# A four-layer Macaron block on one Trainium2 core: the mixed layers' factor sums, bias additions and order of chunks

## The reference

```python
x = L0_attn_x
x = x + 0.5 * _L0_ffn_ref(_layernorm(x), W_r, b_r, W1, b1, W2, b2)      # routed: ffn_a
x = x + _L0_attn_ref(_layernorm(x), ...)                                # latent attention
x = x + 0.5 * _L0_ffn_ref(_layernorm(x), W_r, b_r, W1, b1, W2, b2)      # routed: ffn_b
x = x + 0.5 * _L1_ffn_ref(_layernorm(x), factors, bias)                 # mixed: mix_a
x = x + _L1_attn_ref(_layernorm(x), Wq, Wk, Wv, Wo)                     # attention
x = x + 0.5 * _L1_ffn_ref(_layernorm(x), factors, bias)                 # mixed: mix_b

def _layernorm(x, axis=-1, eps=1e-05):
    m = jnp.mean(x, axis=axis, keepdims=True)
    v = jnp.var(x, axis=axis, keepdims=True)
    return (x - m) / jnp.sqrt(v + eps)

def _L1_ffn_ref(x, factors, bias):           # factors: 8 x 256 x 256
    mixed = jnp.einsum('btd,rde->bte', x, factors)
    return mixed / math.sqrt(8) + bias
```

## Time and profile before

| | |
|---|---|
| median of 3 runs | 1937.31 us (1936.6 to 1941.16) |
| profiled execution, its own time | 1940.07 us |
| its span, first to last instruction | 1938.3 us |
| TensorE busy | 1717.4 us (89%) |
| VectorE busy | 1531.0 us (79%) |
| ScalarE busy | 1181.3 us (61%) |
| GpSimd busy | 983.2 us (51%) |
| mean granted clock of TensorE | 0.932 of full speed |

### The profile page before, as it was taken

The page is one execution under the profiler, slowest core; times in us unless marked ns, Lnnn a source line. Parts: engine busy times, 40 slices in busy tenths (PEclk is TensorE's granted clock), DMA queues, the critical chain, the costliest instruction groups (busy, mean ns, idle before and its releaser), DMA issues. The chain is left out here.

```text
span 1938.3 us, 27188 instructions
## 1 busy us (share of the span) xinstructions
PE 1717.4 (89%) x9368; PEld 1003.3 (52%) x9368; DVE 1531.0 (79%) x2236; ACT 1181.3 (61%) x2043; POOL 983.2 (51%) x820
## 2 busy tenths in 40 slices
PE   4667999999999999999999998565979899999986
PEld 3554555556565555565565654455644344444445
DVE  6772888998997988988889887677566988888816
ACT  1045787777776777778777776111325377778760
POOL 0004799897896997988979988002412000000110
PEclk8776999999999999999999999677987699999998
DMA  3100000000000000000000000111330200110001
GB/s 101 55 24 24 1 1 1 15 1 12 3 1 15 1 1 15 1 15 1 1 7 1 1 1 1 47 47 38 76 77 2 34 1 2 21 15 2 2 1 44
DMA packets 26697, 34.34 MB, mean 18 GB/s; under 512 B 5312, under 2 KB 19648, under 8 KB 26432
## 3 DMA queue, kind: packets, MB, share of 16 engines
q1 hardware_dynamic: 25360, 31.28, 6.8%
q10 hardware_dynamic: 1200, 1.31, 0.2%
HBM read 26.03 MB, written 6.29 MB: 17 GB/s over the span
## 5 line engine op out<-in xcount | busy, mean ns | idle before, releaser
L1208 POOL TENSOR_TENSOR lath_summed<-lath_summed,lath_held 128x512 f32<-128x512 f32 x392 | 524.0, 1337 | 54.4 <-ACT lath_held L1114 27.5
L1925 ACT ACTIVATE atth_probs<-atth_score 128x512 f32<-128x512 f32 (+3 forms) x640 | 293.2, 539 | 141.4 <-PE atth_score L1844 139.8
L1279 DVE TENSOR_TENSOR lath_held<-lath_held,lath_shift 128x1024 f32<-128x1024 f32 (+2 forms) x352 | 331.5, 970 | 24.6 <-PE lath_shift L1027 15.1
L1108 ACT ACTIVATE lath_held<-lath_score 128x1024 f32<-128x1024 f32 (+2 forms) x352 | 283.6, 828 | 105.5 <-DVE lath_largest L1232 52.1
L1114 ACT ACTIVATE lath_held<-lath_held 128x1024 f32<-128x1024 f32 (+2 forms) x352 | 292.6, 861 | 50.3 <-DVE lath_held L1279 48.6
L1884 DVE TENSOR_REDUCE atth_maxima<-atth_slot 128x2 f32<-128x1024 f32 (+3 forms) x288 | 287.3, 1043 | 42.1 <-PE atth_slot L1827 41.1
L1014 PE MATMUL lath_out<-lath_held,lat_latent 128*64 128x512 f32 (+1 forms) x1152 | 303.0, 591 | 7.9 <-ACT lath_held L1114 4.3
L998 PE MATMUL lath_score<-lath_query_hi,lat_key_hi 128*128 128x512 f32 x576 | 246.8, 428 | 22.4 <-ACT lath_held L1108 17.2
L1772 POOL TENSOR_SCALAR_AFFINE_SELECT atth_probs<-atth_probs 128x512 f32<-128x512 f32 x64 | 40.6, 635 | 419.1 <-ACT atth_probs L1925 419.1
L1003 PE MATMUL lath_score<-lath_query_hi,lat_key_lo 128*128 128x512 f32 x576 | 231.2, 401 | 0.0
L1232 DVE TENSOR_TENSOR lath_largest<-lath_score,lath_largest 128x1024 f32<-128x1024 f32 (+2 forms) x240 | 211.7, 882 | 17.5 <-PE lath_score L1003 12.5
(11 more groups left out here) (345 smaller groups left out, 2894.6 us busy)
## 6 DMA issues: line engine op xcount, KB each, us to landing
att_first_query<-att_scratch SPq DMA_DIRECT2D x12, 256.0 KB, 8.9
atth_query<-att_scratch SPq DMA_DIRECT2D x12, 256.0 KB, 9.7
ffn_a_w<-in_L_ffn_W SPq DMA_DIRECT2D x2, 1024.0 KB
lat_raw_out<-in_L_attn_w_out SPq DMA_DIRECT2D x8, 256.0 KB, 2.7
lat_rope<-in_c_rope_feature SPq DMA_DIRECT2D x1, 2048.0 KB, 10.7
ffn_b_w<-in_L_ffn_W SPq DMA_DIRECT2D x2, 1024.0 KB, 7.1
mix_a_factors<-in_L_ffn_factors SPq DMA_DIRECT2D x8, 256.0 KB, 4.2
att_scratch<-attp_high SPq DMA_DIRECT2D x4, 512.0 KB, 2.8
```

What stands on the lines that cost most here:

```text
L1108: nc.scalar.activation(part_columns(slot(n), tiles, q0), part_columns(score_bank[n % 2], tiles, q0), ACT.Copy)\
L1208: nc.gpsimd.tensor_tensor(total, total, slot(n)[:, i, :], ALU.add).then_inc(s["tiles_summed"], 1)
L1279: nc.vector.tensor_tensor(columns, columns, added, ALU.subtract)\
L1925: nc.scalar.activation(probs[:, step % PROB_STEPS, h, q0:CH], score_bank[u % 3][:, q0:CH], ACT.Exp, scale=SCALE1)\
```

## The change

The factor and bias loads move to the end of SyncE's list in the second routed stage (`if not first` there means ffn_b). That stage gets a list for GpSimd: it waits until all 16 tiles are scaled and all factors are there, sums the factors in seven instructions, waits for the bias and halves it. The first mixed stage has no loads and no sums any more.

In both mixed stages GpSimd adds half the bias to x, a chunk (four tiles, 128x1024) an instruction, once all 16 tiles are scaled. Its second operand is the one bias row tile, read four times. VectorE's adding of a chunk's products waits for it (`biased`). `Norm.vector` is split into `statistics` and `scale(chunks)`, and `Turn.vector` and `Turn.tensor` take a choice of chunks, so that scalings, copies and additions on VectorE, and turns and products on TensorE, stand chunk by chunk.

```diff
 class Turn:
-    def vector(self, dve):
-        for b in range(0, 2 * NCH, 2):
+    def vector(self, dve, chunks=range(NCH)):
+        for b in (ND * c for c in chunks):
...
-    def tensor(self, pe):
+    def tensor(self, pe, chunks=range(NCH)):
         nc, n = self.core.nc, len(self.banks)
-        for b in range(2 * NCH):
+        for b in (ND * c + d for c in chunks for d in range(ND)):
...
 class Norm:
+    def scale(self, chunks):
+        for t in (TPC * c + i for c in chunks for i in range(TPC)):
+            self.core.nc.vector.tensor_scalar(self.xn[:, t, :], self.core.x[:, t, :], self.moments[:, t, 0:1], self.rstd[:, t:t + 1],
+                                              ALU.subtract, ALU.mult).then_inc(self.xn_ready, 1)
...
 def routed_ffn_stage(core, tag, first=False):
+                if not first:
+                    for r in range(RANK):
+                        sp.dma_start(factors[:, r], inp["L1_ffn_factors"][r].rearrange("(k p) e -> p k e", p=P)).then_inc(s["factors_loaded"], 16)
+                    sp.dma_start(core.half_bias[:], inp["L1_ffn_bias"].partition_broadcast(P)).then_inc(s["bias_loaded"], 16)
+
+            @block.gpsimd
+            def _(pool):
+                if not first:
+                    pool.wait_ge(norm.xn_ready, NT)
+                    pool.wait_ge(s["factors_loaded"], 16 * RANK)
+                    for r in range(1, RANK):
+                        if r > 1:
+                            pool.wait_ge(s["summed"], r - 1)
+                        nc.gpsimd.tensor_tensor(core.mixed[:], factors[:, 0] if r == 1 else core.mixed[:], factors[:, r], ALU.add).then_inc(s["summed"], 1)
+                    pool.wait_ge(s["bias_loaded"], 16)
+                    nc.gpsimd.tensor_scalar(core.half_bias[:], core.half_bias[:], 0.5, None, ALU.mult).then_inc(s["summed"], 1)
+                    pool.wait_ge(s["summed"], RANK)
...
 def mixed_ffn_stage(core, tag, out=None):
             @block.gpsimd
             def _(pool):
-                if first:
-                    for r in range(1, RANK):
-                        pool.wait_ge(factors_loaded, 16 * RANK)
-                        earlier = factors[:, 0] if r == 1 else core.mixed[:]
-                        if r > 1:
-                            pool.wait_ge(summed, r - 1)
-                        nc.gpsimd.tensor_tensor(core.mixed[:], earlier, factors[:, r], ALU.add).then_inc(summed, 1)
+                pool.wait_ge(norm.xn_ready, NT)
+                for c in range(NCH):
+                    tiles = x[:, TPC * c:TPC * (c + 1), :]
+                    nc.gpsimd.tensor_tensor(tiles, tiles, core.half_bias[:].unsqueeze(1).broadcast_to([P, TPC, DIM]), ALU.add).then_inc(biased, 1)
 
             @block.vector
             def _(dve):
-                norm.vector(dve, Link(core, dve, f"{tag}_dve_link"))
...
+                def add(c):
+                    dve.wait_ge(biased, c + 1)
+                    for b in (2 * c, 2 * c + 1):
+                        dve.wait_ge(mixed_done, b + 1)
...
+                norm.statistics(dve, Link(core, dve, f"{tag}_dve_link"))
+                norm.scale((0, 1))
+                for c in range(2, NCH):
+                    norm.turn.vector(dve, (c - 2,))
+                    norm.scale((c,))
+                norm.turn.vector(dve, (2,))
+                add(0)
+                norm.turn.vector(dve, (3,))
+                for c in range(1, NCH):
+                    add(c)
...
             @block.tensor
             def _(pe):
-                norm.tensor(pe)
-                if first:
-                    pe.wait_ge(summed, RANK - 1)
-                for b in range(NT // 2):
-                    norm.turn.wait_chunk(pe, 2 * b // TPC)
...
+                norm.turn.tensor(pe, (0, 1))
+                mix(0)
+                norm.turn.tensor(pe, (2,))
+                mix(1)
+                norm.turn.tensor(pe, (3,))
+                mix(2)
+                mix(3)
```

More of the change, by code:

```diff
@@ L293, in routed_ffn_stage @@
         table_scratch = sb("table_scratch", [P, 1])
+        factors = None if first else sb("factors", [P, RANK, ND, DIM])
         bank = [ctx.enter_context(nc.psum_tensor(f"{tag}_bank{i}", [P, CH], F32)) for i in range(8)]
@@ L473, in mixed_ffn_stage @@
 def mixed_ffn_stage(core, tag, out=None):
-    nc, x, inp = core.nc, core.x, core.inp
+    nc, x = core.nc, core.x
     with ExitStack() as ctx:
-        first = not core.mixed_ready
-        core.mixed_ready = True
-        factors = core.sb(f"{tag}_factors", [P, RANK, ND, DIM], F32, ctx) if first else None
         xn = core.sb(f"{tag}_xn", [P, NT, DIM], F32, ctx)
@@ L507, in _ @@
[L507 to L518 removed]
+                def add(c):
+                    dve.wait_ge(biased, c + 1)
+                    for b in (2 * c, 2 * c + 1):
+                        dve.wait_ge(mixed_done, b + 1)
+                        pair = x[:, 2 * b:2 * b + 2, :]
+                        nc.vector.scalar_tensor_tensor(pair, bank[4 + b % 4][:].rearrange("p (t d) -> p t d", d=DIM),
+                                                       0.5 / float(np.sqrt(RANK)), pair, ALU.mult, ALU.add).then_inc(added, 1)
@@ L526, in _, with mix @@
             def _(pe):
-                norm.tensor(pe)
-                if first:
-                    pe.wait_ge(summed, RANK - 1)
-                for b in range(NT // 2):
-                    norm.turn.wait_chunk(pe, 2 * b // TPC)
-                    if b >= 4:
-                        pe.wait_ge(added, b - 3)
-                    for i in range(2):
-                        t = 2 * b + i
-                        for k in range(ND):
-                            last = nc.tensor.matmul(bank[4 + b % 4][:, i * DIM:(i + 1) * DIM], xn_t[:, k, t * P:(t + 1) * P],
-                                                    core.mixed[:, k, :], start=(k == 0), stop=(k == ND - 1))
-                    last.then_inc(mixed_done, 1)
+                def mix(c):
+                    norm.turn.wait_chunk(pe, c)
+                    for b in (2 * c, 2 * c + 1):
+                        if b >= 4:
+                            pe.wait_ge(added, b - 3)
+                        for i in range(2):
+                            t = 2 * b + i
+                            for k in range(ND):
+                                last = nc.tensor.matmul(bank[4 + b % 4][:, i * DIM:(i + 1) * DIM], xn_t[:, k, t * P:(t + 1) * P],
+                                                        core.mixed[:, k, :], start=(k == 0), stop=(k == ND - 1))
+                        last.then_inc(mixed_done, 1)
+                norm.turn.tensor(pe, (0, 1))
[5 more added lines that the diff above has]
+                mix(3)
             @block.sync
             def _(sp):
-                if first:
-                    for r in range(RANK):
-                        sp.dma_start(factors[:, r], inp["L1_ffn_factors"][r].rearrange("(k p) e -> p k e", p=P)).then_inc(factors_loaded, 16)
-                    sp.dma_start(core.half_bias[:], inp["L1_ffn_bias"].partition_broadcast(P)).then_inc(bias_loaded, 16)
                 if out is not None:
```

29 lines of the change are left out of this document (7 added, 22 removed).

## The result

| | before | changed |
|---|---|---|
| median of 5 interleaved runs each | 1936.60 us (1934.89 to 1941.16) | 1925.92 us (1922.80 to 1938.66) |
| ratio of the times, 95% interval | | 0.9949 (0.9927 to 0.9971) |
| profiled execution, own time | 1940.07 us | 1925.92 us |
| its span | 1938.3 us | 1924.2 us |
| mean granted clock of TensorE | 0.932 | 0.937 |

The changed kernel is faster, and its time lies 2.0 us under the forecast of 1927.9. The ratio makes 9.9 us of 1936.6, with an interval from 5.6 to 14.1 us. The changed kernel run once more among the experiments gave 0.9928 (0.9907 to 0.9949), 14.0 us of 1940.87. The forecast was 9.4.

What follows compares the result with a forecast made beforehand. TensorE was taken as the bound in the last mixed layer, delayed in the first by GpSimd's sums holding VectorE's scaling. 10.2 + 0.4 saved less 1.2 lost gave 9.4 off 1937.31, so 1927.9 us, range 1924.5 to 1934.

Steps and rivals of the forecast that it cites:

- The collision in the first mixed layer: First mixed layer: without GpSimd's sums holding VectorE's scaling, products end at T+21.4 instead of T+31.6, 10.2 us saved.
- The new order in the last layer: Last mixed layer: turning and multiplying without a gap ends products at T+21.4 instead of T+21.8, 0.4 us saved (-0.1 to 0.8).
- the low clock: Mixed layers: TensorE's clock may still be low when products begin, 0 to 0.9 us lost, 0.4 taken.
- The routed layer: Second routed layer: the moved sums and halving cost 1.2 us, between 0 and 3.4.
- the widening copy: Routed layer: sums may hold VectorE's copy widening the router weights, on which TensorE waits; up to 1.27 us, 0.3 taken.
- The halving: Routed layer: GpSimd's halving of the bias falls among the comparisons; between nothing and 0.85 us, 0.5 taken.
- the tail that I charged: Routed layer: the seventh sum's end holds the first of 16 comparisons for 0.4 us.
- Four bias additions on GpSimd: Mixed layers: four additions of 128x1024 take 2.5 us each, in time for VectorE, with no collision charged.
- (1): Rival, routed layer: factors land late and all sums fall among the comparisons, 9.7 us lost, 1936.4 us; chance 0.09.
- (2): Rival, mixed layers: bias additions hold VectorE's copies and additions after all, 6.6 us saved, 1930.7 us; chance 0.05.
- (3): Rival, mixed layers: GpSimd needs time (middle 7.2 us) before additions run again, 3.4 us saved, 1933.9 us; chance 0.06.
- (4): Rival, mixed layers: GpSimd slow at the repeated bias input; at 5.5 us each, 6.2 us slower, 1943.5 us; chance 0.04.

Runs made afterwards that it cites:

- order_only: Kernel before with the chunk-by-chunk order and GpSimd's bias additions, loads and sums left in the first mixed layer; ratio 0.9970 to the kernel before.
- sums_moved: Changed kernel's loads, sums and halving in the routed layer, but mixed layers in the old order with bias on VectorE; ratio 0.9958 to the kernel before.
- halve_on_scalar: Changed kernel with the halving of the bias on ScalarE instead of GpSimd; ratio 0.9926 to the kernel before.
- sums_after_scaling: Kernel before with one wait more: GpSimd's sums stay in the mixed layer, behind the scaling of all 16 tiles; ratio 1.0009 to the kernel before.
- before_again: Kernel before, unchanged, profiled once more in one run; its last mixed layer ended at T+21.8.
- before_third: Kernel before, unchanged, a third profile from one run; its last mixed layer ended at T+21.8.
- sums_moved_again: The sums_moved kernel, unchanged, profiled once more in one run; its mixed layers ended one at T+23.5, one at T+21.8.
- bias_on_vector: Changed kernel with the four bias additions of 128x1024 on VectorE instead of GpSimd; ratio 0.9924 to the kernel before.
- sums_on_compares: Changed kernel with GpSimd's sums started only after the first of the routed layer's 16 comparisons; ratio 0.9954 to the kernel before.
- split_statistics: On top of halve_on_scalar, both mixed layers' statistics taken in halves so TensorE starts after eight tiles; ratio 0.9874 to the kernel before.
- factors_first: On top of split_statistics, factors loaded ahead of the routed layer's expert weights and router weights widened before scaling; ratio 0.9902 to the kernel before.

## Why the prediction was right

- **The collision in the first mixed layer.** Forecast 10.2 us, measured 10.13. It is shown from both sides: with the sums away no scaling was over 412 ns; with the sums back (order_only) 1490 ns came back, and the layer ended at T+29.7. The 10.13 holds the new order too: with the sums alone moved the layer ended at T+23.7, 8.0 us earlier.
- **The new order in the last layer.** Forecast 0.4, measured 1.12, outside its own bounds (-0.1 to 0.8). The products began at T+4.9, not T+5.1, and products and turns took 15.7 us, not 15.9. The 0.4 charged for the low clock was not paid in this layer (last product T+20.6), and was about 0.8 in the first (T+21.5). I had taken the old order's end as fixed at T+21.8; sums_moved shows that it can be T+23.7, while no profile of the new order with the sums moved ended after T+21.5. So the order, which I gave 0.8 us in two layers, is worth 3 to 6 in the runs. The ratios give 14.0 - 8.1 = 5.9, but their intervals overlap (0.9907 to 0.9949 and 0.9942 to 0.9974). The traces give 2.2 + 3.0 = 5.2 with the first profile of sums_moved, and 2.0 + 1.1 = 3.1 with the second, which had a late rise of the clock in the first layer only.
- **The routed layer.** Forecast 1.2 lost, measured 0.83: the sums came 0.7 later than reckoned, missed the widening copy (0.3 charged) and put a tail of 0.43 us on a comparison (0.4 charged). The halving took 2.62 us, not under 0.85, but fell beside comparisons and cost two of them 0.14 us each (0.5 charged). So three comparisons were over 1.3 us, where I had written one or two. The seventh sum can cost more than the tail that I charged: where it begins beside the first comparison, the second is held for 1.0 us (2286 ns in halve_on_scalar).
- **Four bias additions on GpSimd.** Forecast 2.5 us each, measured 2.36; they collide with nothing: beside them a copy takes VectorE 0.69 us and two additions 1.28, where the earlier trace rows has 1.28 for two copies and 0.69 for an addition.
- **The start of the first mixed layer.** I had no term for it. From the last addition of the routed layer to T it took 9.70 to 9.71 us in all five profiles with loads and sums in the mixed layer, and 9.26 to 9.28 in the seven with them in the routed layer and the statistics whole. So these 0.44 us belong to the change; why the barrier is shorter was not tried.
- **The rest.** The sum of the terms was 9.4; this pair of traces gives 10.13 + 1.12 + 0.44 - 0.83 = 10.9. What the pair has beyond that (3.2 of 14.1) is in code that the change leaves alone. The timed 9.9 has an interval of 4 us either way, and in it such differences are contained, so that it meets 9.4 within 0.5 is in part luck; what bears the mechanism out is the 10.13 in the layer itself.

The rivals: (1) did not come about, and would have cost 7.4 us, not 9.7, had the factors landed late: 1.0 us for each sum, not 1.27, and 0.3 for the halving, not 0.85. (2) is refuted by VectorE's rows beside the additions. (3) is refuted by the first addition at 1309.93, right behind the last scaling (1308.47 + 1.37 = 1309.84). (4) is refuted by 2.36 us for each.

## What to carry to other kernels

A median of 411 ns and a greatest of 1491 in one group is the sign of two engines on one resource: move one of them to a stretch where the other waits or reads PSUM, and look at what is next to it there, since sums_after_scaling only changed the partner. When a row of work has its own start-up chain on one engine (here statistics, 8.1 us with TensorE idle), splitting it in halves can be worth more than reordering behind it: here 6.5 us against 3 to 6. What an interleaving is worth is read from several profiles of the old order, not from one, if a clock that rises at varying times decides it.

## What the runs showed that I had not expected

- **Who loses in a collision depends on lengths and starts.** Sums of 128x512 on GpSimd take 1.26 us alone, and also beside scalings of 0.41 us (which become up to 1.49). Beside comparisons of 1.28 us they take 2.13 us, and comparisons up to 2.32: there each engine waits for the instruction that the other has under way.
- **The clock of TensorE.** From its first instruction in a mixed layer to the rise from 0.50 to full: 3.4 us in the earlier trace rows, 4.0 in the same layer of before_again and before_third, 5.2 and 3.5 in the changed kernel, 8.5 and 8.4 in sums_moved, 8.2 and 4.0 within one profile in sums_moved_again.
- **The unchanged attention varies.** From the last product of the first mixed layer to the first statistic of the last one it took 567.1 to 569.6 us in the three profiles of the kernel before, 566.0 in both of the changed kernel, 569.0 and 569.9 in those of sums_moved, 572.4 in bias_on_vector, and 562.0 to 562.6 in sums_on_compares, halve_on_scalar, split_statistics and factors_first. Its code is the same. Profiles of one kernel lie closer together than the kernels do, so something ahead of the attention may set it; what does was not tried. It also puts a limit on the ratios: two kernels can differ by several us in a part that their edit does not touch.
- **GpSimd's first halving** took 2.62 us for 128x256, right behind its configuration, where an addition of that size takes 0.85. It always ran beside comparisons, so how much of it is waiting is not shown.
